# Layer norm columns of the expert stage's first four tiles, made by ScalarE inside the scan's last batch

## What is computed

```
x = x + tanh(g_xattn[0]) * mamba(ctx, layernorm(x))       # B = 4 batches of 512 positions, 16 states
x = x + tanh(g_ffn[0])   * experts(layernorm(x))          # 16 experts, top 2, and a shared expert
x = x + tanh(g_xattn[1]) * attention(layernorm(x), ctx)   # 32 heads
x = x + tanh(g_ffn[1])   * ffn(layernorm(x))              # weights rounded to three values
layernorm(x) = (x - mean(x)) / sqrt(var(x) + 1e-5)        # over the 512 columns of a row
```

## Time and profile before

| | |
|---|---|
| median of three runs | 1639.32 us (1633.78 to 1642.1) |
| the profiled execution | 1637.02 us, its span 1634.9 us (2.1 us lie around the span) |
| mean granted TensorE clock | 0.953 of full speed |
| PE busy | 1471.3 us, 90% of the span |
| DVE busy | 1140.0 us, 70% |
| ACT busy | 978.8 us, 60% |
| POOL busy | 521.0 us, 32% |
| last batch's steps behind its gates | about 396 to 464 us |
| the expert stage's first instruction | 470.6 us |
| last routing step before POOL's scatter | 529.7 us |

### The profile page before, as it was taken

One profiled execution on the slowest core, in us unless ns is written; L12 is line 12 of the kernel. 1 busy time (PEld: TensorE's weight loads), 2 busy tenths in 40 slices (PEclk: granted clock), 3 DMA queues, 4 the chain that ended last, 5 costly groups with the idle time before them and its releaser, 6 DMA issues. The chain is left out here.

```text
span 1634.9 us, 21624 instructions
## 1 busy us (share of the span) xinstructions
PE 1471.3 (90%) x6294; PEld 641.9 (39%) x6309; DVE 1140.0 (70%) x1687; ACT 978.8 (60%) x1537; POOL 521.0 (32%) x332
## 2 busy tenths in 40 slices
PE   5689988889969799999998588899999999999899
PEld 2334434344434344444443233332333333244444
DVE  7989999999977222222223458788999999638975
ACT  3999999999923011111112342387787878878764
POOL 0679788698950710000004336515000000000000
PEclk7889979999989999999999789999999999999999
DMA  5202102012571574467425516354323232120344
GB/s 179 69 21 57 47 20 72 20 33 65 197 252 69 205 161 162 151 206 263 168 84 167 174 59 189 100 142 156 93 71 90 72 89 74 58 103 1 65 111 121
DMA packets 133478, 181.30 MB, mean 111 GB/s; under 512 B 46451, under 2 KB 80627, under 8 KB 132387
## 3 DMA queue, kind: packets, MB, share of 16 engines
q1 hardware_dynamic: 111878, 132.48, 27.4%
q0 software_dynamic: 6624, 23.14, 4.7%
q10 hardware_dynamic: 14912, 24.89, 4.5%
HBM read 109.29 MB, written 54.92 MB: 100 GB/s over the span
## 5 line engine op out<-in xcount | busy, mean ns | idle before, releaser
L1809 DVE TENSOR_REDUCE a_mx<-a_s 128x2 f32<-128x1024 f32 x256 | 303.5, 1219 | 33.5 <-PE a_s L1923 30.1
L265 POOL TENSOR_TENSOR m_hs<-m_hs,m_C 128x1024 f32<-128x1024 f32 x128 | 302.4, 2382 | 76.4 <-DVE m_hs L476 75.9
L476 DVE TENSOR_TENSOR_SCAN m_hs<-m_dA,m_d 128x512 f32<-128x512 f32 x256 | 293.5, 1198 | 10.0 <-PE m_d L622 8.9
L622 PE MATMUL m_d<-ident_sb,m_dBuT 128*128 128x128 f32 x1024 | 162.9, 292 | 24.2 <-DVE m_hs L476 16.7
L622 PEld LDWEIGHTS m_d<-ident_sb,m_dBuT 128*128 128x128 f32 x1024 | 117.6, 147 | 154.2 <-DVE m_hs L476 79.6
L371 ACT ACTIVATE m_dA<-m_dt,m_negA 128x512 f32<-128x512 f32 x256 | 168.1, 710 | 6.5 <-DVE m_hs L476 4.4
L1252 PE MATMUL e_gu<-e_w,e_xgT 128*128 x376 | 169.1, 592 | 0.0
L349 ACT ACTIVATE m_dBuT<-m_dtuT,m_BT 128x512 f32<-128x512 f32 x241 | 157.7, 710 | 0.1
L1923 PE MATMUL a_s<-ring_sb 96*128 96x512 bf16 x512 | 150.8, 384 | 4.2 <-DVE a_mx L1809 3.0
L918 ACT ACTIVATE e_sg<-e_gu 128x256 f32<-128x256 f32 x47 | 18.0, 384 | 222.9 <-PE e_gu L1252 222.9
L637 PE MATMUL m_y<-m_hs,m_fold 128*64 128x512 f32 x512 | 145.5, 649 | 0.4 <-POOL m_hs L265 0.4
(11 more groups left out here) (336 smaller groups left out, 2441.1 us busy)
## 6 DMA issues: line engine op xcount, KB each, us to landing
e_w<-in_ex_gu SPq DMA_DIRECT2D x16, 1024.0 KB, 6.5
ring_sb<-qk_dram SPq DMA_DIRECT2D x64, 192.0 KB, 3.1
xg_dram<-zeros_sb SPq DMA_DIRECT2D x2, 6016.0 KB, 28.3
e_xg<-xg_dram ACTq DMA_DIRECT2D x47, 256.0 KB, 2.6
yg_dram<-e_yo ACTq DMA_DIRECT2D x47, 256.0 KB, 2.0
m_C<-c_dram SPq DMA_DIRECT2D x64, 128.0 KB, 2.9
m_dt<-m_dt SPq DMA_DIRECT2D x64, 128.0 KB, 2.3
e_w<-in_ex_dn SPq DMA_DIRECT2D x16, 512.0 KB, 8.3
```

The lines of the kernel that those rows point to most:

```text
L265: pool.tensor_tensor(hs[:, J % RH], hs[:, J % RH], C2[:, N % RC].unsqueeze(1).broadcast_to([P, 2, L]), ALU.mult).then_inc(s_hc, 1)
L476: dve.tensor_tensor_scan(hs[:, J % RH, h], dA[:, j % RA], pd[j % RD][:], 0.0, ALU.mult, ALU.add)\
L622: last = pe.transpose(pd[j % RD][:, t * P:(t + 1) * P], dBuT[:, N % 2, t, g], ident[:])
L1809: dve.tensor_reduce(mx[:, r % 2, h * TB + 2 * c:h * TB + 2 * c + 2], psc[c][:], AX.X, ALU.max)\
```

## The change

Tiles 0 to 3 of x_sb are final during the last batch. The change makes their two layer norm columns there.

- ACT, in its steps s = 8 to 11 of the last batch, sums each tile by an Identity activation with an accumulator output, into `lead[:, 0]`; at s = 12 it scales the four sums by -1/512 (Copy), which gives minus the mean. In steps 13 to 16 it squares each tile with minus the mean as bias, accumulated into `lead[:, 1]`. At s = 18 it takes the root of (sum / 512 + epsilon), and calls the exp and log table back. The elementwise results go to a new buffer `junk` that nobody reads.
- DVE, in its step s = 22 of the last batch, behind the scan and ahead of the scaled input of L459, makes the reciprocal and the product -mean/std.
- POOL sets epsilon once, at the start of the program.
- In the expert stage ACT normalises tiles 0 to 3 at once, from `lead`; the statistics, variance, root and columns of group 0 are gone. The semaphore counts of groups 1 to 3 go down by one, and DVE's order of the first part is rearranged.

```
@@ scan stage, POOL
             pool.memset(zeros[:], 0.0).then_inc(s_z0, 1)
+            pool.memset(lead[:, 2], EPS).then_inc(s_eps, 1)
@@ scan stage, ACT
+            def lead_step(s):
+                if 8 <= s < 12:
+                    if s == 8:
+                        act.wait_ge(s_add, E4)
+                    else:
+                        act.wait_ge(s_lead, s - 8)
+                    act.activation(junk[:], x_sb[:, s - 8], ACT.Identity, accum_out=lead[:, 0, s - 8:s - 7])\
+                        .then_inc(s_lead, 1)
+                if s == 12:
+                    act.wait_ge(s_lead, 4)
+                    act.activation(lead[:, 0], lead[:, 0], ACT.Copy, scale=-1.0 / D).then_inc(s_lead, 1)
+                if 13 <= s < 17:
+                    act.wait_ge(s_lead, s - 8)
+                    act.activation(junk[:], x_sb[:, s - 13], ACT.Square, bias=lead[:, 0, s - 13:s - 12],
+                                   accum_out=lead[:, 1, s - 13:s - 12]).then_inc(s_lead, 1)
+                if s == 18:
+                    act.wait_ge(s_lead, 9)
+                    act.wait_ge(s_eps, 1)
+                    act.activation(lead[:, 1], lead[:, 1], ACT.Sqrt, scale=1.0 / D, bias=lead[:, 2, 0:1]).then_inc(s_lead, 1)
+                    act.preload_act_table_set("natural_log_exp_and_others")
...
+                if b == B - 1:
+                    lead_step(s)
                 if s == 5 and p < B:
@@ scan stage, DVE
                 if b >= 1 and 28 <= s < 32:
                     add(b - 1, s - 28)
+                if b == B - 1 and s == 22:
+                    dve.wait_ge(s_lead, 10)
+                    dve.reciprocal(lead[:, 1], lead[:, 1]).then_inc(s_lead, 1)
+                    dve.wait_ge(s_lead, 11)
+                    dve.tensor_tensor(lead[:, 0], lead[:, 0], lead[:, 1], ALU.mult).then_inc(s_lead, 1)
                 if J % E4 == 2 and SHARED <= J // E4 + 1 < B * PAIRS:
@@ expert stage, ACT
-            root(0)
-            normalise(0)
+            for t in range(TB):
+                act.activation(xn[:, t], x_sb[:, t], ACT.Identity, scale=lead[:, 1, t:t + 1], bias=lead[:, 0, t:t + 1])\
+                    .then_inc(s_xn, 1)
             root(1)
             copy_logits(0)
             normalise(1)
@@ expert stage, DVE
-            statistics(0, 1, 2, 3)
-            variance(0)
-            columns(0)
             statistics(4, 5)
-            copy_x(0, 1, 2, 3)
-            statistics(6, 7)
+            copy_x(0)
+            statistics(6)
+            copy_x(1)
+            statistics(7)
+            copy_x(2)
             variance(1)
+            copy_x(3)
+            columns(1)
             statistics(8, 9)
-            columns(1)
             copy_x(4, 5)
```

More of the change, by code:

```diff
@@ L33, with mamba @@
 LN_READY = 2 * NT + 3
-def mamba(nc, x_sb, ident, identb, tg, a, c_dram, xg_dram, zeros, s_zero):
+def mamba(nc, x_sb, ident, identb, tg, a, c_dram, xg_dram, zeros, s_zero, lead):
     G8 = 2 * E4
@@ L60, in mamba @@
         w_xp = sb("w_xp", [P, E4, RX])
+        junk = sb("junk", [P, D])
         w_dt = sb("w_dt", [R, D])
@@ L101, in mamba @@
         s_cst = sem("c_stored")
+        s_eps = sem("epsilon_set")
+        s_lead = sem("first_layer_norm_steps")
         s_d2 = [sem(f"dt_doubled{i}") for i in range(E4)]
@@ L709, with moe @@
 GR = 8
-def moe(nc, x_sb, ident, tg, a, xg_dram, yg_dram, s_zero, early, s_early, attn, s_tab, slot, wk, tab_dram):
+def moe(nc, x_sb, lead, ident, tg, a, xg_dram, yg_dram, s_zero, early, s_early, attn, s_tab, slot, wk, tab_dram):
     with ExitStack() as ctx:
@@ L922, in root @@
             def root(c):
-                act.wait_ge(s_var, c + 1)
+                act.wait_ge(s_var, c)
                 act.activation(rstd[:, c * TB:(c + 1) * TB], rstd[:, c * TB:(c + 1) * TB], ACT.Sqrt).then_inc(s_sd, 1)
             def normalise(c):
-                act.wait_ge(s_nm, c + 1)
+                act.wait_ge(s_nm, c)
                 for t in range(c * TB, (c + 1) * TB):
@@ L1023, in columns @@
                 r = rstd[:, c * TB:(c + 1) * TB]
-                dve.wait_ge(s_sd, c + 1)
+                dve.wait_ge(s_sd, c)
                 dve.reciprocal(r, r).then_inc(s_ln, 1)
@@ L2531, in build @@
         s_zero = ctx.enter_context(nc.semaphore("slots_zeroed"))
-        mamba(nc, x_sb, ident, identb, tg, a, c_dram, xg_dram, zeros, s_zero)
+        lead = ctx.enter_context(nc.sbuf_tensor("lead_sb", [P, 3, TB], F32))
+        mamba(nc, x_sb, ident, identb, tg, a, c_dram, xg_dram, zeros, s_zero, lead)
         early = ctx.enter_context(nc.sbuf_tensor("early_sb", [P, KD * T], F32))
         attn = ctx.enter_context(nc.sbuf_tensor("attn_sb", [P, 2 * B, TB, D // 2], F32))
-        moe(nc, x_sb, ident, tg[:, 2:3], a, xg_dram, yg_dram, s_zero, early, s_early, attn, s_tab, slot, wk, tab_dram)
+        moe(nc, x_sb, lead, ident, tg[:, 2:3], a, xg_dram, yg_dram, s_zero, early, s_early, attn, s_tab, slot, wk, tab_dram)
         mark = ctx.enter_context(nc.semaphore("first_after_moe"))
```

## The result

The changed kernel took a median of 1642.37 us in 20 runs, beside 1633.93 us in 20 runs of the kernel before. The ratio is 1.0041, with a 95% interval of 1.0021 to 1.0061: some 6.7 us slower (3.4 to 10); the two medians themselves are 8.4 us apart. The forecast was +5.7 us, within 0.5%; the upper end of the interval lies a little beyond that.

A forecast was written before the change was run, and what follows sets the result against it. Three engines (DVE, POOL, PE) were read as full in the last batch and ACT nearly so, its lead over DVE deciding; seam 0 plus scan stage 5.7 gave +5.7 us, from 1639.3 to 1645.0, 8-in-10 range 1639 to 1652.

The forecast's parts named there:

- The seam, 0 us: Expert stage's start: PE begins some 3.8 us earlier but still waits for the shared weights' DMA, so the gain is 0.
- a shared block sooner than 12.8 us: Sign of error: the shared block beginning less than 12.8 us after the expert block's start.
- The clock's term: Shared block at the expert stage's start: PE's clock may rise sooner or later, bounds -1.0 and +0.5 us, taken as 0.
- ACT's work, 8.4 us: Last batch: eight passes 5.44 us, small Copy 0.1, root with two table loads 2.85; 8.4 us in all (7.9 to 9.7).
- rival 3: ACT's table switch around the root is dearer, by 2 x 1.28 us: +8.3 us, 1647.6; chance 0.05.
- rival 4: Identity and Square lie outside the exp and log table, two more loads per pass: +5.7 + 21.6 us, 1666.6; chance 0.04.
- The slack, 2.7 us at step 120: Last batch: ACT's k = 6 tile is ahead of DVE's scan by 2.7 us at step 120, 0.44 less each group earlier.
- Stage +5.7 us: Last batch: ACT's added 8.4 us less the slack of 2.7 ends the scan stage 5.7 us later (5.2 to 7.0).
- a window below 1.00: Sign of error: a profile window of the last batch after the change shows the granted clock below 1.00.
- Rival 1: PE's clock falls in the last stall, ahead of step 120, losing 3.4 us (2.5 to 4.4): +9.1, 1648.4; chance 0.27.
- the sum for the gap: PE's gap ahead of step 120: 5.7 - 3.2 us plus its usual few tenths, about 2.7 us.
- DVE's columns, 0.4 us: Last batch, s = 22: two small DVE instructions cost about 0.4 us, hidden in the stall ahead of step 120.

The follow-up runs named there:

- The two halves apart: Changed scan stage with the expert stage of before: 1641.84 us, ratio 1.004; changed expert stage alone, tiles 0 to 3 normalised by constants: 1635.28 us, ratio 1.0011.
- the split wait: Second shared weights on their own semaphore, awaited only ahead of first use: on the kernel before 1634.61 us, ratio 0.9999; on the changed kernel 1632.46 us, 0.9989.
- Three doses: ACT's new work in the last batch: root with tables only, scan stage 75.89 us; eight passes only, 80.90; all, the changed kernel itself, 83.12.
- the first experiment: Changed kernel with the expert stage of before, the early columns unused: 1641.84 us against 1635.91, ratio 1.004; scan stage 82.51 us.
- the kernel with the passes alone: Changed kernel's scan stage without the root, its table loads and DVE's columns, with the expert stage of before: scan stage 80.90 us in one execution.
- the steps behind the last decay: Changed kernel, ACT's new steps moved after its loop, DVE's columns ahead of its last add: 1607.83 us, ratio 1.0008; with the split wait 1600.38 us, 0.9963.

## Why the prediction was right

**The seam, 0 us: right.** The two halves apart show it, and the split wait shows that the cover was the DMA's wait and nothing behind it. The landing was 12.5 us behind the start, 0.2 sooner than before. By the letter a shared block sooner than 12.8 us is one of the forecast's own signs of being wrong; that sign was too sharp, since with the whole wait in place the shared block began 11.3 to 12.8 us behind the start in the profiles here. The clock's term there, taken as 0 between -1.0 and +0.5, came out at +0.2 (6.74 against 6.56); that it is 0 is luck in part, as the same eight matmuls took 3.70 to 6.74 us behind the whole wait in the other profiles.

**ACT's work, 8.4 us: right**, at 8.39. A sum was 0.62 (0.63 forecast), a square 0.70 (0.73), the root with its tables 2.91 (2.85). No drain stands behind a table load: 435.24 + 1.28, root at 436.54. The Trainium skill's 2.66 us per switch (page "ScalarE: Activation LUTs", section "What ACT_TABLE_LOAD costs") is not what these rows show, and rival 3 falls with it; so does rival 4, there being no other load.

**The slack, 2.7 us at step 120 and 0.44 less for each group before: right.** Three doses (2.9, 5.5, 8.4 us) gave 0.3, 3.1 and 5.7 us, the last without its slow transposes.

**Stage +5.7 us: low by 1.8.** The forecast took the clock to stay whole in the last batch, and named a window below 1.00 as a sign that it is wrong. Rival 1, with a chance of 0.27, says that it falls, and it fell in all three profiles that hold the whole of ACT's work where the change puts it. So the forecast left out a term that is there each time. The gap ahead of step 120 was 4.0 us and not 2.7: behind the stall before, PE got ahead of DVE (its transposes came 2.03 us apart, 434.06 to 440.15, while a step costs DVE 2.24), which the sum for the gap did not count. The clock then cost 0.4 + 1.4 us, not the 2.5 to 4.4 of rival 1. Its slow stretch was about 7 us, as the rival allows, but 1.6 of them lay in the gap, where PE does nothing, and behind it 1.8 us were lost in 5.2, 0.35 of each against the rival's 0.43. Forecast and rival 1 bracket the result: a stage of +7.5 (+6.9 in the first experiment) between 5.7 and 9.1, and the median by some 6.7 us, or 8.4 between the medians. That the number fits as well as it does is so far luck: the ratio's interval does not tell 5.7 from 7.5. The absolute figure of 1645.0 rested on a median of three runs, and that of 20 is 5.4 us lower. The shares summed up for "slower by over 0.5%" give 0.29 and not 0.31.

**DVE's columns, 0.4 us, hidden: right in the sum, wrong in the price.** They cost 2.3 to 2.6 us a pair where nothing covers them, the waits for PE included. In the changed kernel the scaled input behind them ended at 444.58, and ACT's tile only at 446.22, so the stall hid this too; with a smaller dose on ACT it would have shown.

Left open: when the clock falls in these gaps. A gap of 2.97 us ahead of step 112 was followed by half the clock in the changed kernel, and one of 2.98 in the kernel with the passes alone was not. A gap of 1.8 us near the batch's end was followed by a fall in three kernels (passes alone, and both with the steps behind the last decay) and not in five others, the kernel before among them, with the same instructions around it. All three ran on one chip and none of the five did, so the chip is a rival to chance here, and whether the steps on ACT play a part was not tested.

## What to carry to other kernels

An engine at 95% busy (9.19 of 9.63 us) is full for a burst: ask how far it is ahead of its consumer, in us at each hand-over; work up to that lead is free, the rest comes out one for one, and where it makes PE wait, PE's clock may fall as well. Ahead of making something earlier, look what the next instruction in that queue waits for: here the early columns alone gave nothing at the seam, the split of one semaphore gave 2.3 to 3.0 us, and with it the early columns were worth 5.9. And look for the idle stretch of the same engine (18 us behind the last decay) before its busy one.

## What the hardware showed that I had not expected

- A VectorE product of two on-chip operands of only four columns lasted 2.11 to 2.36 us in nine of fourteen cases, until the GpSimd product beside it ended (0.16 to 0.34 in three, 1.69 in two); a one-input reciprocal took 0.17 in the middle of such a product.
- An accumulating activation of 128x512 costs the engine only 0.1 us more than one without (0.62 against a pace of 0.50, 0.70 against 0.60): the read of 0.19 us overlaps both neighbours. With nothing but such passes in a row, each waiting for the one before, a pass took 0.76 and 0.85 us.
- The wait that is removed at the seam of the changed kernel gave back 5.8 us by itself and 3.0 more by the clock: the eight matmuls behind it took 6.74 us with the gap of 5.74 and 3.70 without. The gap ahead of them is not all: without any gap they took 5.05 us in the kernel before with the split wait, where the clock was half from 470 to 482, and behind a gap of 1.75 us 3.70 in the kernel with the passes alone.
